# Moving matmul operands 8 and 16 bytes apart in SBUF: attention weights, gate and up weights, attention outputs

## The reference, cut to what matters

```python
x = x + _L0_xattn_ref(_layernorm(x), ctx_4096, ctx_4096, mask, wq, wk, wv, wo, 0)   # keys: the 64 context rows, with RoPE
x = x + _L0_ffn_ref(_layernorm(x), w_gate, w_up, w_down)                            # 512 -> 1376 -> 512, silu(gate) * up, values cut to int8
x = x + _L1_xattn_ref(_layernorm(x), ctx_4096, Wq, Wk, Wv, Wo, q_norm_w, k_norm_w)  # keys: 64 context and 64 latent rows, RMS norm on q and k
x = x + _L1_ffn_ref(_layernorm(x), gamma, beta, w1, b1, w3, b3)                     # 512 -> 512 -> 512, rows fake-quantised
```

## Time and profile before

| | before |
|---|---|
| median of 3 runs | 1532.07 us (1531.17 to 1535.59) |
| profiled execution, its own time | 1531.07 us |
| its span | 1529.3 us |
| TensorE matmuls busy | 1475.2 us, 96% |
| TensorE weight loads busy | 1276.0 us, 83% |
| VectorE busy | 950.2 us, 62% |
| ScalarE busy | 597.5 us, 39% |
| GpSimd busy | 564.3 us, 37% |
| matmuls | 11536, each with a weight load |

### The profile page before, as it was taken

One profiled execution on the slowest core, in us unless ns is written; L12 is line 12 of the kernel. 1 busy time (PEld: TensorE's weight loads), 2 busy tenths in 40 slices (PEclk: granted clock), 3 DMA queues, 4 the chain that ended last, 5 costly groups with the idle time before them and its releaser, 6 DMA issues.

```text
span 1529.3 us, 28684 instructions
## 1 busy us (share of the span) xinstructions
PE 1475.2 (96%) x11536; PEld 1276.0 (83%) x11536; DVE 950.2 (62%) x1983; ACT 597.5 (39%) x1434; POOL 564.3 (37%) x468
## 2 busy tenths in 40 slices
PE   6899999999999998999899999999999999999986
PEld 5788888888888876887798899898899989889973
DVE  7666665665666675666866456455655645565588
ACT  4313222222222234442355353444435344443556
POOL 4535354443536423652134122222312222231258
PEclk9999999999999999999899999999999999999998
DMA  7111020111112003320112011110101011010201
GB/s 198 42 29 50 21 69 29 42 30 41 43 29 65 8 20 97 80 60 21 42 29 70 1 43 29 28 43 21 50 1 42 29 29 43 14 57 1 80 5 56
DMA packets 84302, 64.45 MB, mean 42 GB/s; under 512 B 7280, under 2 KB 71024, under 8 KB 84176
## 3 DMA queue, kind: packets, MB, share of 16 engines
q1 hardware_dynamic: 83600, 62.47, 14.2%
q10 hardware_dynamic: 576, 0.20, 0.1%
HBM read 60.56 MB, written 2.10 MB: 41 GB/s over the span
## 4 chain that ended last, share of the span: by engine, by line
PE 47%; DVE 2%; POOL 1%; issue 1%; ACT 0%; DVEq 0%; ACTq 0%; POOLq 0%
PE att_proj L70 35%; PE att_att L800 4%; PE att_sco L758 4%; PE att_att L775 2%; PE att_proj L722 1%; PE att_sco L737 1%; POOL ffn_y L476 0%; DVE ffn_top L428 0%; DVE ffn_y L470 0%; POOL x_rows L414 0%; PE att_att L242 0%; DVE ffn_y L424 0%; DVE stats L383 0%; DVE x_rows L1053 0%; ACT ffn_y L435 0%
## 5 line engine op out<-in xcount | busy, mean ns | idle before, releaser
L148 POOL TENSOR_TENSOR att_w_lo<-w_raw,att_w_hi 128x512 fp32r<-128x512 f32 x160 | 206.7, 1317 | 179.5 <-ACT att_w_hi L143 172.0
L1416 POOL TENSOR_TENSOR att_probs<-att_probs,att_total 128x512 f32<-128x512 f32 x64 | 82.8, 1294 | 455.8 <-DVE att_total L1037 341.7
L70 PE MATMUL att_proj<-att_w_hi,kv_hi 128*128 128x256 f32 x768 | 223.4, 291 | 10.2 <-DVE kv_lo L260 10.2
L70 PE MATMUL att_proj<-att_w_hi,kv_lo 128*128 128x256 f32 x768 | 218.3, 284 | 0.0
L70 PE MATMUL att_proj<-att_w_lo,kv_hi 128*128 128x256 f32 x768 | 218.3, 284 | 0.0
L70 PE MATMUL att_proj<-kv_hi,att_w_hi 128*128 128x512 f32 x512 | 207.6, 406 | 1.5 <-DVE kv_lo L251 1.5
L70 PE MATMUL att_proj<-att_w_hi,att_o_hi 128*128 128x512 f32 x512 | 205.0, 400 | 1.9 <-issue 1.9
L70 PE MATMUL att_proj<-kv_lo,att_w_hi 128*128 128x512 f32 x512 | 201.8, 394 | 0.0
L70 PE MATMUL att_proj<-kv_hi,att_w_lo 128*128 128x512 f32 x512 | 201.5, 393 | 0.0
L70 PE MATMUL att_proj<-att_w_lo,att_o_hi 128*128 128x512 f32 x512 | 199.8, 390 | 0.0
L70 PE MATMUL att_proj<-att_w_hi,att_o_lo 128*128 128x512 f32 x512 | 199.5, 390 | 0.0
(11 more groups left out here) (167 smaller groups left out, 2740.2 us busy)
## 6 DMA issues: line engine op xcount, KB each, us to landing
w_raw<-in_wq SPq DMA_DIRECT2D x64, 256.0 KB, 2.9
w_raw<-in_wo SPq DMA_DIRECT2D x64, 256.0 KB, 2.8
w_raw<-in_wk SPq DMA_DIRECT2D x16, 256.0 KB, 3.0
w_raw<-in_wv SPq DMA_DIRECT2D x16, 256.0 KB, 3.3
w_raw<-in_gate_t SPq DMA_DIRECT2D x10, 256.0 KB, 2.9
w_raw<-in_up_t SPq DMA_DIRECT2D x10, 256.0 KB, 3.1
w_raw<-in_down_t SPq DMA_DIRECT2D x10, 256.0 KB, 3.0
spare<-in_ctx_t SPq DMA_DIRECT2D x4, 512.0 KB, 5.7
```

The source lines that it names most:

```text
L70: ins = eng.matmul(out, a, b, start=(first and n == 0), stop=(last and n == 3 * len(terms) - 1))
L148: eng.tensor_tensor(self.lo[:, chunk], self.raw[:, n % RAW_SLOTS], raw(self.hi[:, chunk]), ALU.subtract)\
L1416: eng.tensor_tensor(probs[:, u % 2, 0:n], probs[:, u % 2, 0:n], total[:, u % 2, 0:n].unsqueeze(2).broadcast_to([P, n, KL]), ALU.mult)\
```

## The change

No instruction is added, removed, moved, or given another shape; both programs have 13,870 instructions in the same order, and differ in the addresses of operands alone.

- `att0_w_hi` and `att0_w_lo` become one tile, whose two halves begin 16 bytes past its start; the same for `att1`. Weights so begin 48 past a multiple of 64 (att0 at 117808, att1 at 50736), where the columns begin 32 past one: 16 bytes off.
- `gu_hi` and `gu_lo` begin 4 values, 16 bytes, further into the space of `kv_lo`; the streamed columns in `kv_hi` stay.
- `o_hi` and `o_lo` become one tile. In `att0` they begin at its start, 185408, a multiple of 64: 16 bytes off the weights and 32 off the columns, if both are taken modulo 64. In `att1` they begin 24 bytes in, at 129080, which is 56 past a multiple of 64: 8 bytes off the weights. There the former 32 bytes of `pad` go.
- What is allocated behind these tiles moves by 32 or 64 bytes (`q_cols`, `k_cols`, `v_rows`, `probs`, `probs_t` in one or both attentions, and small tiles). The columns, `ffn_down_hi`, `ffn_down_lo` and `ffn_hid` stay.

```diff
     def place(self, nc, scope):
-        self.hi, self.lo = (scope.enter_context(nc.sbuf_tensor(f"{self.tag}_w_{n}", [P, CHUNKS, BANK], F32R))
-                            for n in ("hi", "lo"))
+        n, ahead = CHUNKS * BANK, 4
+        both = scope.enter_context(nc.sbuf_tensor(f"{self.tag}_w_hi_lo", [P, 2 * n + 2 * ahead], F32R))
+        self.hi, self.lo = (both[:, ahead + i * n:ahead + (i + 1) * n].rearrange("p (c n) -> p c n", n=BANK) for i in range(2))
...
-        if not rope:
-            sb("pad", [P, 8])
         q_cols = sb("q_cols", [P, 4, NBH, 2, S])
         k_cols = sb("k_cols", [P, NB * KL])
         v_rows = sb("v_rows", [P, NB * KL // P, HD])
         k_rows = sb("k_rows", [P, NBH * KL // P, HD])
-        o_hi, o_lo = (sb(n, [P, GROUP, NBH, S], F32R) for n in ("o_hi", "o_lo"))
+        size, ahead = GROUP * NBH * S, 0 if rope else 6
+        o_both = sb("o_hi_lo", [P, 2 * size + 8], F32R)
+        o_hi, o_lo = (o_both[:, ahead + i * size:ahead + (i + 1) * size].rearrange("p (g b s) -> p g b s", g=GROUP, s=S)
+                      for i in range(2))
...
-        n = 4 * KT * P
-        self.gu_hi, self.gu_lo = (flat_lo[:, i * n:(i + 1) * n].rearrange("p (a b k n) -> p a b k n", a=2, b=2, k=KT)
-                                  for i in range(2))
+        n, ahead = 4 * KT * P, 4
+        self.gu_hi, self.gu_lo = (
+            flat_lo[:, i * n + ahead:(i + 1) * n + ahead].rearrange("p (a b k n) -> p a b k n", a=2, b=2, k=KT)
+            for i in range(2))
```

## The result

The changed kernel is slower: 1541.42 us median of 4 runs (1540.47 to 1544.28), against 1532.38 us (4 runs, 1531.17 to 1535.59) for the kernel before on the same chip. The ratio is **1.006**, its 95% interval 1.0048 to 1.0072: 9.0 us lost where 34 us of gain were forecast.

What follows compares the result with a forecast made beforehand. TensorE, busy 96%, was taken to bound the kernel through its matmul distances. Half of a 68 us excess (27.6 at 256 columns, 40.3 at 512), 34 us, was taken off, giving 1498 us; range 1464 to 1541.

Steps and rivals of the forecast that it cites:

- the sum of distances is the time: Whole kernel: time is the distances between TensorE's matmul starts plus its short waits, 54 us idle; gains pass in full.
- the down products kept theirs: Sign to check in the feed-forward part: the down products, whose tiles stay, must keep their distance.
- cost of the writers: ScalarE and GpSimd writing the shifted tiles: hidden by TensorE's work, so nothing; without that cover at most 21 us.
- belongs to one weight load, not to the columns streamed: fp32r matmuls: the same 11 to 12 ns excess at 256 and 512 columns is tied to each weight load.
- its floor, 108 ns: 256-column products: transposes' weight-load distance of 108 ns taken as floor, so the measured 120.0 has 12 ns too much.
- I take half of the upper bound, 34 us: Moved-operand matmuls, 2304 of 256 and 3600 of 512 columns: half of the 68 us excess goes; chance of part 0.33.
- rival "slower": 512-column products settle elsewhere or never, 5.5 ns each if as at a burst's start; 1549 us in all, chance 0.22.
- would be a lucky best: Argument against the slower rival: equal first addresses, the placement before the change, would have to be a lucky best.
- The unsettled starts of bursts: Burst starts: 232.2 ns at 512 columns, 118.9 at 256, later settling; read as the excess depending on the reads' timing.
- Nothing changes: Rival: the 11 ns are a charge of the fp32r load, so placement does nothing; 1532 us, chance 0.25.
- the rule on two ports: Skill rule: TensorE has two independent SBUF read ports, loading weights steals nothing from the running matmul; time stays 1532 us.

Runs made afterwards that it cites:

- after: The changed kernel itself, with all parts of the change, against the kernel before: 1541.42 us median against 1532.38, ratio 1.006.

## Why the prediction was wrong

- **That the sum of distances is the time** held. Busy time and span rose by the same 13 us, no wait was added, the down products kept theirs, and no cost of the writers showed.
- **The excess "belongs to one weight load, not to the columns streamed".** As a charge for the load this failed. Half the load took nothing off it (229.5 ns), and half the load time with bf16 left 225. At the lower granted clock it is gone (426.7 ns). That it was 12 ns at 256 columns as well was weak support: its floor, 108 ns, was taken from transposes, a bound of another kind, and the lowest distance that any run reached is 113.3.
- **The step that failed: "I take half of the upper bound, 34 us"**, resting on the thought that two reads whose first addresses differ should meet less often. Measured for the kinds that the term named: `project` +9.7, `q_job` +4.0 and gate and up +3.2 us, where the term had -20; `kv_job` -2.9, where it had -14. The size and, at 512 columns, the sign were wrong. It did not behave like a conflict of the two first addresses that an offset takes away; moving them put the 512-column products into longer patterns, 233 to 237 ns.
- **The rival "slower"** had the mechanism in kind: the 512-column products settle elsewhere. Its price was 5.5 ns for each; measured were 16.9 us over the 3600 products (3.2 + 9.7 + 4.0), 4.7 ns each. That the two lie so close is luck: the price was that of bursts that never settle, and after's settle, in `project` sooner than before's. Against it the prediction held that equal first addresses "would be a lucky best". For the placement of before that is what they are at 512 columns: no kernel settled lower.
- **The unsettled starts of bursts** The earlier trace rows were rightly read as a sign that the distance isn't fixed. But they show the way into a repeating pattern, not a conflict that an offset removes: in the burst of `project` at 441.83 us the kernel before has distances of 229, 234, 236, 224, 231, 235, 229, 232 and 231 ns and then keeps to 227, 226, 227, while after is in 234, 239 by the fifth distance.
- **Nothing changes**, the rival of the rule on two ports, is refuted. Moving only the loaded operand of gate and up by 16 bytes took each matmul from 226.7 to 233.3 ns. The Trainium skill, "TensorE: Matmul & The Clock Gate", part 2, has loads steal nothing from the running matmul; the trace disagrees as far as that would make the place of the loaded operand indifferent.

The Trainium skill, "SBUF — State Buffer", on cachelines, has lines of 16 bytes and a penalty for each crossing to a new one. That operands spread over twice the bytes stream some 10 ns slower agrees in kind; but the page also calls a step of up to 8 bf16 values free, and here a step of two took 225 ns where contiguous values took 215. No run here measured a line, and by that rule alone a common move by 16 bytes of both operands should leave `project` at 226.7, where 230 was measured.

**What stays open** is why an offset leads to one pattern and not to another, and which further differences count. Level operands gave 226.7, 229.3, 230, 231 and 233.7 ns, in kernels that differ in the gaps between tiles by multiples of 64 bytes, or in a common 16 or 32 bytes; a common 16 bytes with nothing else changed wasn't run. How a burst begins plays a part, as after's `q_job` shows, but was varied in no run of its own. Other candidates are the gap between the `hi` and `lo` of one operand, differences modulo more than 64, and tiles that other engines use at the time. What the two reads do inside TensorE or the memory was only argued.

## What to carry to other kernels

In a stage where one engine has no idle time, read the distance from start to start of each kind of its instructions, and test a placement on each kind apart: the same 16 bytes gained 1 to 7 ns on 256-column products and cost up to 10 on 512-column ones, and nothing on some of them. Don't price a difference between two measured rates as a conflict that placement removes until one kernel has shown that it depends on what you think causes it. And when a placement is tried, keep the gaps between all other tiles, or the comparison measures them too. Look at the spread of the runs before reading one trace: with weights and outputs 16 off, the trace was 10 us faster than the median.

## What the runs showed of the hardware

- The starts of matmuls in a long burst fall into a repeating pattern whose mean changes with where the operands lie: for fp32r with 512 columns from 226.5 to 237.3 ns, with 256 columns from 113.3 to 126, in programs that do the same work. Moving the loaded operand alone by 16 bytes took gate and up from 226.7 to 233.3.
- One placement can have two patterns in one execution: 226.7 ns for bursts behind transposes, 233 for most others (after, `q_job`, second attention).
- At a granted clock of 0.50 the distance of 512 columns was 426.7 ns, level and 16 bytes off alike.
- The distance didn't follow the offset smoothly: 16, 20 and 24 bytes gave 233.3, 226.7 and 237 ns for `project`, the last in the second attention, in kernels that also differ otherwise.
- A shift of all memory by 32 or 64 bytes changed nothing (1.0002 both times), while all operands moved by 32 with 64 bytes more per tile were slower (1.0054).
- Loading 64 columns instead of 128 made 512-column matmuls no faster, 229.5 against 226.7 ns in one run.
- bf16 values read from every second place stream 512 columns in 225 ns, contiguous ones in 215.
